# Seven quarter products in place of eight for the second matrix product of six batches, all batches unrolled

## The chip, the core and the metric

The kernel runs on one core of a Trainium2 chip. The metric is device time in microseconds (us), and lower is better. TensorE (PE) does the matrix products, VectorE (DVE) and ScalarE (ACT) the elementwise work, SyncE (SP) issues nearly all transfers, and GpSimd (POOL) prepares a few constants.

## The reference, cut to what matters

```
y    = x @ weight[adapter_ids]^T            # per batch: 256 x 1024 times 1024 x 1024
base = y @ W_up^T                           # 256 x 1024 times 1024 x 1024
top1 = argmax(y @ gate_w^T + expert_bias)   # one of 4 experts for each token
d    = (y @ lora_A^T, the 8 columns of top1) @ lora_B^T of top1
out  = x + base + d
```

There are 8 batches of 256 tokens and a hidden size of 1024. Everything is float32.

## The kernel before, in words

TensorE takes its operands as fp32r, a rounded form. To keep float32 accuracy each operand is split into hi (the rounded copy, made by ACT) and lo (the rest, made by DVE as raw minus hi), and a product is three: hi times hi, hi times lo, lo times hi. So each of the two large products of a batch costs three passes.

**First product.** For each of 8 blocks of 128 output features (`c`) it takes one 512 KB block of the batch's adapter weights from a ring of four raw blocks `w_raw` (split into `w_hi`, `w_lo`, rings of four too). For each of 8 slices `k` it issues a matmul of 512 columns (w_hi times x hi and x lo, L474) and one of 256 (w_lo times x hi, L476) into one of two PSUM banks. Then ACT copies one half of the bank out (`y_small`, L292), DVE adds the other (`y_full`, L408), ACT rounds it (`y_hi`, L296) and DVE takes the rest (`y_lo`, L413). Between these, ACT and DVE split the weights that come next (L271, L352) and, after the last block, the next batch's x (L257, L339). TensorE may go on with block `c` when `y_full` of block `c - 2` is done and the weights of `c` are split.

**Second product.** For each of two tiles of 128 tokens (`t`) three PSUM banks hold 366, 366 and 292 output columns; the third also holds 2 x 36 columns of lora_A and the gate (hi and lo), appended to `up_hi`. `bank_ab` (L485) feeds the first two with matmuls of 366 columns, `bank_c` (L494) the third with 364, 328 and 292. From the third bank DVE chooses the expert and builds `z_parts` (`choose`), TensorE transposes it (L502), ACT copies that back (`zT`, L313), and `add_lora` (L509) adds the LoRA term to each bank. DVE adds the banks to the rows of x (`finish`, L400) and SP stores them.

Batch 0 is written out, also splitting w_up once; batches 1 to 7 run in a loop. Every engine works its own list in order and waits on semaphores at fixed places; that order is written by hand. SP's list matters below: a load of a raw block waits until the block that it overwrites has been split by DVE, and everything behind it in SP's list waits too.

Of the kernel before, what the change touches and what calls it, by code (L numbers as in the profile page):

```python
# [8 lines left out]

# [1 line left out]

# [2 lines left out]

P = 128
F32 = mybir.dt.float32
F32R = mybir.dt.float32r  # L20
I32 = mybir.dt.int32
ALU = mybir.AluOpType
AX_X = mybir.AxisListType.X


def build(nc, xT, x, ids, w, w_up, gl, lora_b, bias, out):
    B, S, H = x.shape
    KC = H // P
# [7 lines left out]
    NW = H + 2 * GL  # L36
    RING = 4
    HALVES = 2
    HK = KC // HALVES
    XQ = 4  # L40
    XK = KC // XQ
    XD = 2
    QUARTERS = 4
    QK = KC // QUARTERS
    WARM = 18
    LAST = (2, 1, 0)

    UP_EARLY = OC // 2

    CUT = (NW // 3 + 1) // 2 * 2  # L50
    BANK_C = H - 2 * CUT
    STEPS = 8
    assert T == 2 and 4 * ER == P and BANK_C + 2 * GL <= 512 and B >= 3

    with ExitStack() as ctx:
# [19 lines left out]
        def sem(name):  # L75
            return ctx.enter_context(nc.semaphore(name))

        w_raw = sb("w_raw", [P, RING, KC * P])
        w_hi = sb("w_hi", [P, RING, KC * P], F32R)
        w_lo = sb("w_lo", [P, RING, KC * P], F32R)  # L80
        x_raw = sb("x_raw", [P, KC, S])
        x_hilo = sb("x_hilo", [P, KC, 2 * S], F32R)
        up_hi = sb("up_hi", [P, OC, NW], F32R)
        up_raw, up_lo = sb_over("up_raw", "up_lo", [P, OC, H])
        gl_raw = sb("gl_raw", [P, OC, GL])
        y_small = sb("y_small", [P, 2, S])
        y_full = sb("y_full", [P, 2, S])
        y_hi = sb("y_hi", [P, OC, S], F32R)
        y_lo = sb("y_lo", [P, OC, S], F32R)
        rows = sb("rows", [P, T, H])  # L90
        lb_raw = sb("lb_raw", [P, H])
        lb_parts = sb("lb_parts", [P, H], F32R)
        warm_f, warm = sb_over("warm_f", "warm", [P, 2 * S])
        bias_sb = sb("bias_sb", [P, E])
        rank = sb("rank", [P, E])
        eye_f = sb("eye_f", [P, P])
        eye = sb("eye", [P, P], F32R)
        zlo = sb("zlo", [P, T, GL])
        zg = sb("zg", [P, T, GL])
        lg = sb("lg", [P, T, E])  # L100
        lmax = sb("lmax", [P, T])
        score = sb("score", [P, T, E])
        smax = sb("smax", [P, T])
        zm = sb("zm", [P, T, ER])
        z_parts = sb("z_parts", [P, T, P], F32R)
        zT = sb("zT", [P, T, P], F32R)

        ps_y = [ctx.enter_context(nc.psum_tensor(f"ps_y{i}", [P, 512], F32)) for i in range(2)]
        ps_o = [ctx.enter_context(nc.psum_tensor(f"ps_o{t}", [P, 3, 512], F32)) for t in range(T)]

        x_raw_in = [sem(f"x_raw_in{d}") for d in range(XD)]
        w_raw_in = [sem(f"w_raw_in{s}") for s in range(RING)]
        up_raw_in = [sem(f"up_raw_in{c}") for c in range(OC)]
# [3 lines left out]
        bias_in = sem("bias_in")  # L117
        x_hi_ready = sem("x_hi_ready")
        x_ready = sem("x_ready")
        w_hi_ready = sem("w_hi_ready")  # L120
        w_ready = sem("w_ready")
        up_hi_ready = sem("up_hi_ready")
        up_ready = sem("up_ready")
        gl_hi_ready = sem("gl_hi_ready")
# [3 lines left out]
        warm_step = sem("warm_step")  # L128
        warm_ready = sem("warm_ready")
# [3 lines left out]
        y_done = sem("y_done")  # L133
        y_small_ready = sem("y_small_ready")
        y_full_ready = sem("y_full_ready")
        y_hi_ready = sem("y_hi_ready")
        y_ready = sem("y_ready")
        z_done = sem("z_done")
# [5 lines left out]
        out_ready = sem("out_ready")  # L144
# [3 lines left out]


        @block.sync  # L150
        def _(sp):
            def adapter(b):

                i = sp.value_load(ids[0:1, b:b + 1] if isinstance(b, int) else ids[0:1, bass.ds(b, 1)])  # L154
# [5 lines left out]
            def load_w(b, c, i):  # L160
                if not (isinstance(b, int) and b == 0 and c < RING):

                    sp.wait_ge(w_ready, (b * OC + c - RING + 1) * QUARTERS)
                sp.dma_start(w_raw[:, c % RING, :], w[bass.ds(i * OC + c, 1), :, :].rearrange("a p n -> (a p) n")  # L164
                             ).then_inc(w_raw_in[c % RING], 16)

            def load_x(b, d):
                sp.wait_ge(x_ready, (b - 1) * XQ + (d + 1) * (XQ // XD))
                ks = slice(d * (KC // XD), (d + 1) * (KC // XD))
                sp.dma_start(x_raw[:, ks, :], xT[b, :, ks, :]).then_inc(x_raw_in[d], 16)  # L170

            def load_up(c):
                sp.dma_start(up_raw[:, c, :], w_up[c, :, :]).then_inc(up_raw_in[c], 16)

            def load_rows(b, t):
                if not (isinstance(b, int) and b == 0):

                    sp.wait_ge(stored[t], b * 16 * (t + 1))
                sp.dma_start(rows[:, t, :], x[b, t * P:(t + 1) * P, :]).then_inc(rows_in[t], 16)

            def store_rows(b, t):
                toks = slice(t * P, (t + 1) * P)
                if t == 0:
                    sp.wait_ge(out_ready, b * 6 + 3)
                    sp.dma_start(out[b, toks, :], rows[:, t, :]).then_inc(stored[t], 16)
                else:
                    sp.wait_ge(out_ready, b * 6 + 5)
                    sp.dma_start(out[b, toks, CUT:], rows[:, t, CUT:]).then_inc(stored[t], 16)
                    sp.wait_ge(out_ready, b * 6 + 6)
                    sp.dma_start(out[b, toks, 0:CUT], rows[:, t, 0:CUT]).then_inc(stored[t], 16)  # L190

            i = adapter(0)
            for c in range(RING):
                load_w(0, c, i)
            for c in range(RING, OC):
                load_w(0, c, i)
                load_up(c - RING)
            sp.dma_start(gl_raw[:, :, :], gl[:, :, :]).then_inc(gl_in, 16)
            for c in range(RING, OC):
                load_up(c)  # L200
            for d in range(XD):
                load_x(1, d)
# [3 lines left out]
            i = adapter(1)  # L206
            for c in range(RING):
                load_w(1, c, i)
            for t in range(T):
                load_rows(0, t)  # L210
            with sp.Fori(0, B - 2) as b:
                i = adapter(b + 1)
                for c in range(RING, OC):
                    load_w(b + 1, c, i)
                for d in range(XD):
                    load_x(b + 2, d)
                for t in range(T):
                    store_rows(b, t)
                i = adapter(b + 2)
                for c in range(RING):  # L220
                    load_w(b + 2, c, i)
                for t in range(T):
                    load_rows(b + 1, t)
            i = adapter(B - 1)
            for c in range(RING, OC):
                load_w(B - 1, c, i)
            for t in range(T):
                store_rows(B - 2, t)
            for t in range(T):
                load_rows(B - 1, t)  # L230
            for t in range(T):
                store_rows(B - 1, t)
            for t in range(T):
                sp.wait_ge(stored[t], B * 16 * (t + 1))


        @block.gpsimd
        def _(pool):
# [3 lines left out]
                               base=0, pattern=[[-1, P]], channel_multiplier=1).then_inc(eye_step, 1)  # L242
            for e in range(E):
                pool.memset(rank[:, e:e + 1], float(E - e)).then_inc(rank_ready, 1)

            pool.wait_ge(gl_hi_ready, 1)
            pool.tensor_tensor(up_hi[:, :, H + GL:NW], gl_raw[:, :, :], up_hi[:, :, H:H + GL].bitcast(F32),
                               ALU.subtract).then_inc(gl_ready, 1)


        @block.scalar
        def _(act):
            def x_hi(b, q):
                if not (isinstance(b, int) and b == 0):
                    act.wait_ge(y_done, b * OC)
                act.wait_ge(x_raw_in[q * XD // XQ], (b + 1) * 16)
                act.copy(x_hilo[:, q * XK:(q + 1) * XK, 0:S], x_raw[:, q * XK:(q + 1) * XK, :]  # L257
                         ).then_inc(x_hi_ready, 1)
# [6 lines left out]
            def w_hi_part(b, c):  # L265
                if not (isinstance(b, int) and b == 0 and c < RING):
                    act.wait_ge(y_done, b * OC + c - RING + 1)
                act.wait_ge(w_raw_in[c % RING], (b * (OC // RING) + c // RING + 1) * 16)  # L268
                for h in range(HALVES):
                    part = slice(h * HK * P, (h + 1) * HK * P)  # L270
                    act.copy(w_hi[:, c % RING, part], w_raw[:, c % RING, part]  # L271
                             ).then_inc(w_hi_ready, QUARTERS // HALVES)

            def up_hi_part(c):
                act.wait_ge(up_raw_in[c], 16)
                act.copy(up_hi[:, c, 0:H], up_raw[:, c, :]).then_inc(up_hi_ready, 1)

            def gate_hi():
                act.wait_ge(gl_in, 16)
# [320 lines left out]
```

## Time and profile before

| | |
|---|---|
| median of 3 runs | 389.05 us (388.99 to 389.36) |
| the profiled execution | 389.27 us, its span 387.5 us |
| PE busy | 381.2 us of the span, 2258 matmuls |
| DVE busy | 212.2 us |
| ACT busy | 144.9 us |
| DMA | 63.7 MB, mean 164 GB/s |

The span runs from the first to the last instruction; 1.8 us of the profiled execution lie around it. Busy times of different engines overlap, so they don't add up.

### The profile page before, as it was taken

How to read it: one execution, taken by the hardware profiler on the slowest of the kernel's cores; microseconds unless marked ns; L12 is line 12 of the kernel's file. 1: busy time of each engine (PE TensorE's matmuls, PEld its weight loads, DVE VectorE, ACT ScalarE, POOL GpSimd, SP SyncE). 2: the span in 40 equal slices, each digit the busy share in tenths (PEclk: the TensorE clock that was granted, in tenths of full speed). 3: DMA queues.
4: the chain of work that ended last, by engine and by line, in shares of the span. 5: the costliest groups of instructions: out<-in, count | busy, mean ns of one | idle time of the engine just before them, and what ended most of it. 6: DMA issues, size and time to landing. Idle time of an engine off the chain costs nothing.

```text
span 387.5 us, 6808 instructions
## 1 busy us (share of the span) xinstructions
PE 381.2 (98%) x2258; PEld 356.3 (92%) x2258; DVE 212.2 (55%) x493; ACT 144.9 (37%) x318; POOL 1.7 (0%) x11
## 2 busy tenths in 40 slices
PE   7999999999999999999999999999999999999996
PEld 5789998899988999889998999989998899988996
DVE  4776976463564554735737347455365562664132
ACT  5666905370063701536025440345204461054000
POOL 0000000000000000000000000000000000000000
PEclk9999999999999999999999999999999999999999
DMA  7999459702775118643096332872338703540002
GB/s 244 355 415 292 175 208 297 255 7 102 188 251 210 67 41 246 236 167 108 31 277 201 140 108 75 260 247 68 108 123 262 250 15 108 184 141 0 0 0 110
DMA packets 18921, 63.70 MB, mean 164 GB/s; under 512 B 2272, under 2 KB 3424, under 8 KB 18912
## 3 DMA queue, kind: packets, MB, share of 16 engines
q1 hardware_dynamic: 18624, 62.55, 48.2%
q10 hardware_dynamic: 288, 1.05, 0.8%
q8 instruction: 3, 0.05, 0.1%
q14 instruction: 6, 0.05, 0.0%
HBM read 55.20 MB, written 8.39 MB: 164 GB/s over the span
## 4 chain that ended last, share of the span: by engine, by line
PE 95%; DMA 2%; SPq 1%; DVE 1%; issue 0%; ACT 0%; DVEq 0%; ACTq 0%
PE ps_o L485 34%; PE ps_y L474 30%; PE ps_o L494 15%; PE ps_y L476 15%; PE ps_o L509 2%; DMA w_raw<-w_dram 2%; SPq L154 1%; DVE w_lo L352 1%; SPq L164 0%; PE ps_y L502 0%; ACT w_hi L271 0%; DVE rows L400 0%; DVE y_full L408 0%; DVEq L350 0%; ACTq L268 0%
## 5 line engine op out<-in xcount | busy, mean ns | idle before, releaser
L474 PE MATMUL ps_y<-x_hilo,w_hi 128*128 128x512 f32 x512 | 178.8, 395 | 1.2 <-DVE y_full L408 0.6
L476 PE MATMUL ps_y<-x_hilo,w_lo 128*128 128x256 f32 x512 | 142.3, 278 | 0.0
L474 PEld LDWEIGHTS ps_y<-x_hilo,w_hi 128*128 128x128 f32 x512 | 96.0, 188 | 24.3 <-DVE w_lo L345 1.0
L476 PEld LDWEIGHTS ps_y<-x_hilo,w_lo 128*128 128x128 f32 x512 | 96.3, 188 | 0.0
L352 DVE TENSOR_TENSOR w_lo<-w_raw,w_hi 128x512 fp32r<-128x512 f32 x126 | 80.1, 687 | 7.6 <-ACT w_hi L271 7.2
L485 PE MATMUL ps_o<-up_hi,y_hi 128*128 128x366 f32 x256 | 75.0, 334 | 0.0
L485 PE MATMUL ps_o<-up_lo,y_hi 128*128 128x366 f32 x256 | 74.1, 330 | 0.0
L485 PE MATMUL ps_o<-up_hi,y_lo 128*128 128x366 f32 x256 | 74.0, 330 | 0.0
L271 ACT CAST w_hi<-w_raw 128x512 fp32r<-128x512 f32 x126 | 69.9, 620 | 4.8 <-DMA w_raw<-w_dram 4.7
L292 ACT COPY y_small<-ps_y 128x256 f32<-128x256 f32 x64 | 23.9, 373 | 114.4 <-PE ps_y L476 114.4
L408 DVE TENSOR_TENSOR y_full<-ps_y,y_small 128x256 f32<-128x256 f32 x64 | 27.1, 424 | 64.2 <-ACT y_small L292 64.2
L485 PEld LDWEIGHTS ps_o<-up_lo,y_hi 128*128 128x128 f32 x256 | 47.0, 189 | 0.0
L485 PEld LDWEIGHTS ps_o<-up_hi,y_lo 128*128 128x128 f32 x256 | 46.9, 188 | 0.0
L485 PEld LDWEIGHTS ps_o<-up_hi,y_hi 128*128 128x128 f32 x256 | 45.4, 188 | 0.4
L494 PE MATMUL ps_o<-up_hi,y_hi 128*128 128x364 f32 x128 | 40.9, 329 | 0.0
L494 PE MATMUL ps_o<-up_hi,y_lo 128*128 128x328 f32 x128 | 38.9, 312 | 0.0
L313 ACT CAST zT<-ps_y 128x128 fp32r<-128x128 f32 x16 | 4.3, 267 | 91.5 <-PE ps_y L502 91.5
L494 PE MATMUL ps_o<-up_lo,y_hi 128*128 128x292 f32 x128 | 37.9, 296 | 0.0
L413 DVE TENSOR_TENSOR y_lo<-y_full,y_hi 128x256 fp32r<-128x256 f32 x64 | 27.0, 422 | 15.1 <-ACT y_hi L296 15.1
L400 DVE TENSOR_TENSOR rows<-ps_o,rows 128x366 f32<-128x366 f32 (+1 forms) x48 | 21.5, 506 | 22.3 <-PE ps_o L509 22.3
L296 ACT CAST y_hi<-y_full 128x256 fp32r<-128x256 f32 x64 | 26.0, 406 | 18.8 <-DVE y_full L408 18.8
L377 DVE COPY zlo<-ps_o 128x36 f32<-128x36 f32 x16 | 3.1, 195 | 50.5 <-PE ps_o L494 50.5
(38 smaller groups left out, 198.6 us busy)
## 6 DMA issues: line engine op xcount, KB each, us to landing
w_raw<-w_dram SPq DMA_DIRECT2D x64, 512.0 KB, 4.2
rows<-x_dram SPq DMA_DIRECT2D x16, 512.0 KB, 5.2
x_raw<-xT_dram SPq DMA_DIRECT2D x14, 512.0 KB, 8.1
up_raw<-w_up_dram SPq DMA_DIRECT2D x8, 512.0 KB, 9.6
out_dram<-rows SPq DMA_DIRECT2D x8, 512.0 KB, 8.6
out_dram<-rows SPq DMA_DIRECT2D x8, 329.0 KB, 7.9
out_dram<-rows SPq DMA_DIRECT2D x8, 183.0 KB, 7.0
x_raw<-xT_dram ACTq DMA_DIRECT2D x2, 512.0 KB, 4.3
```

Source lines behind the costliest of these rows:

```text
L271: act.copy(w_hi[:, c % RING, part], w_raw[:, c % RING, part]).then_inc(w_hi_ready, QUARTERS // HALVES)
L292: act.copy(y_small[:, c % 2, :], ps_y[c % 2][:, S:2 * S]).then_inc(y_small_ready, 1)
L296: act.copy(y_hi[:, c, :], y_full[:, c % 2, :]).then_inc(y_hi_ready, 1)
L352: dve.tensor_tensor(w_lo[:, c % RING, part], w_raw[:, c % RING, part], w_hi[:, c % RING, part].bitcast(F32), ALU.subtract).then_inc(w_read ...
L400: dve.tensor_tensor(rows[:, t, part], ps_o[t][:, k, 0:part.stop - part.start], rows[:, t, part], ALU.add).then_inc(out_ready, 1)
L408: dve.tensor_tensor(y_full[:, c % 2, :], ps_y[c % 2][:, 0:S], y_small[:, c % 2, :], ALU.add).then_inc(y_full_ready, 1)
L413: dve.tensor_tensor(y_lo[:, c, :], y_full[:, c % 2, :], y_hi[:, c, :].bitcast(F32), ALU.subtract).then_inc(y_ready, 1)
L474: pe.matmul(ps_y[c % 2][:, :], w_hi[:, c % RING, cols], x_hilo[:, k, :], start=(k == 0), stop=False)
L476: last = pe.matmul(ps_y[c % 2][:, S:2 * S], w_lo[:, c % RING, cols], x_hilo[:, k, 0:S], start=False, stop=(k == KC - 1))
L485: pe.matmul(ps_o[t][:, k, 0:CUT], y[:, c, toks], up[:, c, k * CUT:(k + 1) * CUT], start=(c == 0 and n == 0), stop=False)
L494: last = pe.matmul(ps_o[t][:, 2, 0:end - 2 * CUT], y[:, c, toks], up[:, c, 2 * CUT:end], start=(c == 0 and end == NW), stop=(c == OC - 1 a ...
L509: pe.matmul(ps_o[t][:, k, 0:part.stop - part.start], zT[:, t, :], lb_parts[:, part], start=False, stop=True, skip_group_check=(k == 2)).th ...
```

## The change

w_up (transposed) is seen as four quarters of 512 x 512 (B11, B12, B21, B22), y as four quarters of 128 tokens x 512 features (A11, A12, A21, A22). Batches 0 and 1 (`b < PLAIN`) form the product from eight quarter products, batches 2 to 7 from seven, by Strassen's algorithm in the form with four sums on each side: S1 to S4 are sums of y's quarters, made anew in each batch by DVE, and T1 to T4 sums of w_up's, made once during batches 1 and 2 from quarters that SP loads a second time. Each quarter product is 4 slices of three matmuls, all of 512 columns (`quarter`). The seven share four PSUM banks: what several outputs have in common is accumulated in `ps_u`, which DVE adds to the rows at intermediate states. The small product with lora_A and the gate is one of its own: 16 matmuls of 256 columns with the 72 hi and lo columns as weights (`gates`), and 4 of 36 columns that fold and transpose it (`logits`).

The ring of raw weight blocks shrinks from four to three (`RAWS`), that of the split ones stays four (`RING`). x_raw shares memory with the lo half of `x_hilo`, so the next x is loaded only when the first product is over. All loops are unrolled. No loop is left on any engine.

The core of the diff, with some calls drawn together in one line and comments added on the right; the code that it replaces is printed above:

```
+    RAWS = 3
     RING = 4
+    def splits_at(b, c):
+        if b == 0:
+            return (c + RAWS,) if c + RAWS < OC else ()
+        n = b * OC + c + RING
+        if c < OC - RING or (b == 1 and c < 6) or (b > PLAIN and c < OC - 1):
+            return (n,) if n < BLOCKS else ()
+        return ()
+    def splits_after(b):
+        done = [n for c in range(OC) for n in splits_at(b, c)]
+        first = done[-1] + 1
+        return range(first, min((b + 1) * OC + RING, BLOCKS))
...
SyncE
+            def load_w(n, i):
+                if n >= RAWS:
+                    sp.wait_ge(w_ready, (n - RAWS + 1) * QUARTERS)
+                sp.dma_start(w_raw[:, n % RAWS, :], ...
...
ScalarE
+            def first_product(b):
+                for c in range(OC):
+                    y_small(b, c)
+                    for n in splits_at(b, c):
+                        w_hi_part(n)
+                    if c == 4:
+                        act.wait_ge(y_full_ready, b * OC + Q)
+                        y_hi_part(A11)
+                        if b < PLAIN:
+                            y_hi_part(A21)
...
+            def plain(b):
...
+                g_parts(b)
+                for q in range(XQ):
+                    x_hi(b + 1, q)
+                for n in splits_after(b):
+                    w_hi_part(n)
+                z_back(b)
+            def strassen(b):
...
+                if b > PLAIN:
+                    for n in splits_after(b):
+                        w_hi_part(n)
+                x_hi(b + 1, 0); x_hi(b + 1, 1)
+                g_parts(b)
+                x_hi(b + 1, 2); x_hi(b + 1, 3)
+                if b == PLAIN:
+                    for n in splits_after(b):
+                        w_hi_part(n)
+                z_back(b)
...
VectorE
+            def plain(b):
...
+                g_full(b)
+                g_lo_part(b)
+                for q in range(XQ):
+                    x_lo(b + 1, q)
+                choose(b)
+                for n in splits_after(b):
+                    w_lo_part(n)
+                for i, (t, j) in enumerate(((0, 0), (0, 1), (1, 0), (1, 1))):
+                    add_row(b, t, j, ps_plain[t, j])
+            def strassen(b):
+                y_add(S2, A22, S3, ALU.subtract, slice(Q - 1, Q))
+                y_lo_part(b, 2, S3)
+                y_add(S4, A12, S2, ALU.subtract)
+                y_add(S1, A21, A22, ALU.add)
+                y_lo_part(b, 3, S2)
+                add_row(b, 0, 0, ps_u)                    # product 1 done
+                y_lo_part of A12, S1, A22, S4
+                add_row(b, 1, 1, ps_v)                    # product 2 done
+                if b == PLAIN:
+                    t_lo(T4, 1)
+                else:
+                    for n in splits_after(b):
+                        w_lo_part(n)
+                add_row(b, 1, 0, ps_u)                    # product 3 done
+                x_lo(b + 1, 0); x_lo(b + 1, 1)
+                g_full(b)
+                g_lo_part(b)
+                x_lo(b + 1, 2); x_lo(b + 1, 3)
+                choose(b)
+                add_row(b, 1, 1, ps_u, after=2)           # product 5 done
+                if b == PLAIN:
+                    for n in splits_after(b):
+                        w_lo_part(n)
+                add_row of ps_l, ps_p, ps_v, and at last ps_u
...
TensorE
+            def quarter(ps, p, q, k, start, stop):        # hi*hi, hi*lo, lo*hi, 512 columns each
...
+            def plain(b):
+                for c in range(OC):
+                    term(0, 0, c)
+                    term(0, 1, c)
+                    term(1, 0, c)
+                    if c == Q:
+                        gates(b)
+                    if c == Q + 1:
+                        logits(b)
+                for c in range(Q):
+                    term(1, 1, c)
+                transpose_z(b)
+                for c in range(Q, OC):
+                    term(1, 1, c)
+                    if c == Q + 1:
+                        add_lora(b, 0, 0, ...), (b, 0, 1, ...), (b, 1, 0, ...)
+                add_lora(b, 1, 1, ps_plain[1, 1])
+            def strassen(b):
+                product(b, 1, ps_u, A11, B11, True)
+                product(b, 2, ps_v, S3, T3, True)
+                product(b, 3, ps_u, S2, T2, False)
+                gates(b)
+                product(b, 4, ps_p, A12, B21, True)
+                logits(b)
+                product(b, 5, ps_u, S1, T1, False)
+                product(b, 6, ps_v, A22, T4, False)       # transpose_z after its slice 1
+                add_lora(b, 1, 1, ps_l, True)             # waits for z_back's second copy
+                add_lora(b, 0, 0, ps_p)
+                add_lora(b, 1, 0, ps_v)
+                add_lora(b, 0, 1, ps_u)
+                product(b, 7, ps_u, S4, B22, False, True)
```

Blocks of adapter weights are numbered through, `n = 8 b + c`. `w_hi_part(n)` needs block `n` landed; `w_lo_part(n)` needs that; `load_w(n + 3)` needs `w_lo_part(n)`. By `splits_after`, batches 0 and 2 split four blocks during the second product (8 to 11, and 24 to 27), batch 1 two (18, 19), batches 3 to 6 one each, batch 7 none.

## Rows read from the trace of the kernel before

**Rows 1.** The page's part 1: busy time, share of the span, count.
```profile
PE 381.2 (98%) x2258; PEld 356.3 (92%) x2258; DVE 212.2 (55%) x493; ACT 144.9 (37%) x318; POOL 1.7 (0%) x11
```

**Rows 2.** The page's part 4: who stands on the chain that ended last.
```profile
PE 95%; DMA 2%; SPq 1%; DVE 1%; issue 0%; ACT 0%; DVEq 0%; ACTq 0%
```

**Rows 3.** Windows: first and second product of batches 0, 1, 2 (one missing).
```profile
8.68:32.22 23.54, 22.88 (x129) 19.64 (x129) 17.53 (x33) 15.02 (x33) 0.81 (x1) 1.00 1.01 372
32.22:57.20 24.98, 24.98 (x157) 24.89 (x156) 20.96 (x42) 14.71 (x25) 0.00 (x0) 1.00 0.63 209
57.20:79.59 22.39, 22.39 (x129) 19.44 (x128) 12.49 (x27) 9.21 (x22) 0.00 (x0) 1.00 0.76 251
79.59:103.95 24.36, 24.36 (x153) 24.36 (x152) 13.83 (x37) 7.57 (x16) 0.00 (x0) 1.00 0.31 90
103.95:126.31 22.36, 22.36 (x130) 19.58 (x130) 11.31 (x23) 9.22 (x22) 0.00 (x0) 1.00 0.66 231
```

**Rows 4.** Chain that ended last, second product of batch 1: start, us, what.
```profile
90.82 4.05 PE ps_o L494 x27
...
99.92 4.03 PE ps_o L485 x24
```

**Rows 5.** Timeline of PE: first product of batch 2, pairs 2 and 32.
```profile
104.31 0.40 PE L474 MATMUL ps_y<-x_hilo,w_hi 128*128 128x512 f32 x1
...
114.70 0.40 PE L474 MATMUL ps_y<-x_hilo,w_hi 128*128 128x512 f32 x1
```

**Rows 6.** Timeline of PE, warm-up matmuls: the first ten; the tenth to the seventeenth.
```profile
1.95 4.29 PE L460 MATMUL ps_y<-warm 128*128 128x512 f32 x10 [1.95 <-DVE warm L439]
...
5.84 2.02 PE L460 MATMUL ps_y<-warm 128*128 128x512 f32 x8
```

**Rows 7.** Timeline of PE, second product of batch 1: a transpose and what follows.
```profile
98.35 0.22 PE L502 MATMUL ps_y<-eye,z_parts 128*128 128x128 f32 x1
98.41 0.38 PE L485 MATMUL ps_o<-up_hi,y_hi 128*128 128x366 f32 x1
98.63 0.33 PE L485 MATMUL ps_o<-up_lo,y_hi 128*128 128x366 f32 x1
```

**Rows 8.** Groups of DVE by form: count, busy us, mean ns.
```profile
L408 DVE TENSOR_TENSOR y_full<-ps_y,y_small 128x256 f32<-128x256 f32 x64 | 27.1, 424 | 64.2 <-ACT y_small L292 64.2
L400 DVE TENSOR_TENSOR rows<-ps_o,rows 128x366 f32<-128x366 f32 x32 | 16.3, 533 | 22.3 <-PE ps_o L509 22.3
```

**Rows 9.** Timelines of DVE and ACT in batch 1: splits back to back.
```profile
83.86 2.49 DVE L352 TENSOR_TENSOR w_lo<-w_raw,w_hi 128x512 fp32r<-128x512 f32 x4
...
82.88 4.27 ACT L271 CAST w_hi<-w_raw 128x512 fp32r<-128x512 f32 x8
```

**Rows 10.** Timeline of DVE: first and last of the nine steps of choose.
```profile
94.92 0.20 DVE L377 COPY zlo<-ps_o 128x36 f32<-128x36 f32 x1 [1.56 <-PE ps_o L494]
...
96.73 0.22 DVE L392 TENSOR_TENSOR z_parts<-zm,z_parts 128x64 fp32r<-128x64 f32 x1
```

**Rows 11.** View of w_raw: from issue to landing.
```profile
DMA to landing us min/median/max: 3.1/4.2/13.4
```

**Rows 12.** Timeline of ACT, batch 0: waits for blocks 5, 6 and 7.
```profile
18.12 1.14 ACT L271 CAST w_hi<-w_raw 128x512 fp32r<-128x512 f32 x2 [1.99 <-DMA w_raw<-w_dram]
...
20.66 1.14 ACT L271 CAST w_hi<-w_raw 128x512 fp32r<-128x512 f32 x2 [0.82 <-DMA w_raw<-w_dram]
...
23.22 1.14 ACT L271 CAST w_hi<-w_raw 128x512 fp32r<-128x512 f32 x2 [0.84 <-DMA w_raw<-w_dram]
```

**Rows 13.** Timeline of all engines at the end of the span.
```profile
384.06 0.33 PE L509 MATMUL ps_o<-lb_parts,zT 128*128 128x366 f32 x1
384.43 0.54 DVE L400 TENSOR_TENSOR rows<-ps_o,rows 128x366 f32<-128x366 f32 x1 [2.58 <-PE ps_o L509]
```

More of the change, by code:

```diff
@@ L84, in build @@
[L84 to L89, printed above, removed]
+        x_at = place([P, 2, KC, S])
+        x_raw = nc.alloc_sbuf_tensor_at("x_raw", [P, 2, KC, S], F32, offset=x_at)
+        x_hilo = nc.alloc_sbuf_tensor_at("x_hilo", [P, 2, KC, S], F32R, offset=x_at)
+        up_stage, up_hi = sb_over("up_stage", "up_hi", [P, PARTS, Q, HALF])
@@ L172, in load_up @@
[L172 to L185, printed above, removed]
-                else:
[L187 to L190, printed above, removed]
+            def load_w(n, i):
+                if n >= RAWS:
+                    sp.wait_ge(w_ready, (n - RAWS + 1) * QUARTERS)
+                sp.dma_start(w_raw[:, n % RAWS, :], w[bass.ds(i * OC + n % OC, 1), :, :].rearrange("a p n -> (a p) n")
+                             ).then_inc(w_raw_in[n % RAWS], 16)
@@ L311, in batch, with z_back @@
+            def z_back(b):
                 for t in range(T):
@@ L323, in _ @@
             x_hi(0, XQ - 1)
-            for q in range(XQ // 2, QUARTERS):
+            for q in range(QUARTERS // 2, QUARTERS):
                 first_w_hi(q)
-            for c in range(1, RING):
-                w_hi_part(0, c)
-            batch(0, first=True)
-            with act.Fori(1, B - 1) as b:
-                batch(b)
-            batch(B - 1, last=True)
+            for n in range(1, RAWS):
+                w_hi_part(n)
+            for b in range(B):
+                first_product(b)
+                if b < PLAIN:
+                    plain(b)
+                else:
+                    strassen(b)
@@ L488, in bank_c @@
-            def bank_c(t, c):
-                toks = slice(t * P, (t + 1) * P)
-                terms = [(y_hi, up_hi, NW), (y_hi, up_lo, H), (y_lo, up_hi, H + GL)]
-                for y, up, end in terms if c < OC - 1 else terms[::-1]:
-                    last = pe.matmul(ps_o[t][:, 2, 0:end - 2 * CUT], y[:, c, toks], up[:, c, 2 * CUT:end],
-                                     start=(c == 0 and end == NW), stop=(c == OC - 1 and end == NW))
-                if c == OC - 1:
-                    last.then_inc(z_done, 1)
@@ new lines, in logits, with transpose_z @@
+            def logits(b):
+                if b == 0:
+                    pe.wait_ge(eye_ready, 2)
+                pe.wait_ge(g_ready, b + 1)
+                for t in range(T):
+                    for part in (g_hi, g_lo):
+                        last = pe.matmul(ps_z[:, t * GL:(t + 1) * GL], part[0:2 * GL, t, :], fold[0:2 * GL, :],
+                                         start=(t == 0 and part is g_hi), stop=False, skip_group_check=True)
+                last.then_inc(z_done, 1)
+            def transpose_z(b):
+                for t in range(T):
+                    pe.wait_ge(z_parts_ready, b * T + t + 1)
+                    pe.matmul(ps_y[t][:, 0:P], z_parts[:, t, :], eye[:, :], start=True, stop=True
+                              ).then_inc(zt_done, 1)
@@ L566 @@
+            warm_up()
+            for b in range(B):
+                first_product(b)
+                if b < PLAIN:
+                    plain(b)
+                else:
+                    strassen(b)
 def kernel(x, itok_B_3_7, L0_cond_weight, L0_ffn_W_up, L0_ffn_gate_w, L0_ffn_expert_bias, L0_ffn_lora_A,
```

760 lines of the change are left out of this document (488 added, 272 removed).

## The prediction

> **What bounds the kernel now.** The page's busy times come first: PE is busy for 98% of the span, DVE for 55% [rows 1]. Since matmuls overlap in the records, a busy PE proves nothing yet; the chain that ended last does, with 95% on PE and 2% on DMA [rows 2]. So time changes by what TensorE has to stream and by what makes it wait. The windows give the price of a stage: after batch 0 a first product takes 22.36 to 22.39 us, a second one 24.36, without idle time [rows 3].
>
> What sets PE's pace is the number of columns. 27 matmuls of `bank_c` (mean 328 columns) take 4.05 us, 150 ns each, 24 of 366 columns 4.03 us, 168 ns each [rows 4]. Thirty pairs of 512 + 256 columns take 114.70 - 104.31 = 10.39 us, 346 ns a pair [rows 5]. All lie at 0.45 to 0.46 ns a column. The only matmuls of 512 columns in a row are the last warm-up ones: from 5.84 on, eight take 2.02 us; less the last one's 0.39, seven starts lie 233 ns apart [rows 6]. Two thirds of a pair is 231. I take 232 ns for 512 columns and 116 for 256. A transpose takes 60 ns and makes the next matmul 50 ns longer [rows 7].
>
> **What the seven products are worth.** A Strassen batch issues 7 x 4 x 3 = 84 matmuls of 512 columns (19.49 us), 16 of `gates` (1.86), 4 of `logits` (0.24, at the price of a transpose, since no row shows 36 columns; at 116 ns it would be 0.2 more), 2 transposes with what follows (0.22) and 4 of LoRA (0.93): 22.74 us in place of 24.36. That is 1.62 less, in six batches 9.7 us. The saving is so small because the gate columns rode in `bank_c` for half of that price.
>
> A plain batch has 96 of 512 (22.27) and the same rest (3.25): 25.52 us. Batch 1 gains 1.16 us of work over its 24.36, batch 0 0.54 over its 24.98 [rows 3].
>
> The page "TensorE: Matmul & The Clock Gate" of the Trainium skill (section "Wait — 56ns, not 53.3ns?") puts a matmul at its columns over 2.4 GHz plus 2.5 ns, some 216 ns for 512. The rows show 232, and the measurement decides. By the page's price the two sides would shrink together, to an estimated 20.9 and 22.5 us, and the gain of a batch would be 1.6 again.
>
> **First products.** The matmuls are the same ones and the split ring is as deep. In batch 0 PE lost 0.66 us of 23.54 [rows 3]. There the smaller raw ring moves loads: a w_up block now goes ahead of block 3. Blocks 5, 6 and 7 came 2.5 us apart with a w_up block between them, 1.3 us for 512 KB [rows 12]; two more such blocks ahead of block 7 make it land some 2.6 us later, near 25.7, still before PE wants it at 28.5. But ACT waits for it ahead of `y_small` of block 5, which makes `y_full` late for PE by 0.7 us, about what the shorter list before the first block gives back. I take 0 for batch 0's first product, between -0.7 and +1.5.
>
> **Where PE will wait.** Batches 0 and 2 split four blocks during the second product, but there are three raw buffers. The fourth block can be loaded only when the first of the four is split by DVE, and both engines stand behind it: ACT does `w_hi` of the fourth before `z_back`, whose copies PE needs for `add_lora`. Durations: DVE splits 512 columns in 0.69 us, 0.60 in a row, ACT in 0.62 and 0.52 [rows 9]; a load takes at least 3.1 us [rows 11]; `choose` 2.03 us for one tile [rows 10], I take 2.5 for two in one chain, with more steps.
>
> *Batch 0*, from the end of `gates`: g's four steps 0.16 + 4 x 0.4 + gaps = 1.9 us; the four `x_lo` end at 4.3 (behind ACT's four `x_hi`, begun at 1.4); `choose` 6.8; `w_lo(8)` 8.1; block 11 lands 11.25; `w_hi(11)` 12.4; first zT 12.7. PE in that time has 9 + 18 + 12 + 6 = 45 matmuls of 512 columns (10.4), logits and transposes (0.5): it arrives at 10.9 and waits 1.8 us.
>
> *Batch 2*, from the start of product 1: PE does products 1 to 3 (8.35), gates (10.2), product 4 (13.0), logits, product 5 (16.1). DVE waits for that, adds a row (16.3 to 17.0, by 533 ns for 366 columns [rows 8], 0.69 for 512), and only then does `w_lo(24)` (18.2). Block 27 lands at 21.4, `w_hi(27)` ends at 22.5, the second zT at 23.0. PE has finished product 6 and the transposes at 19.0 and waits 4.0 us. Behind its wait stand the four LoRA matmuls and product 7, and behind them the whole next batch; nothing covers it. If the load took the median 4.2 us [rows 11] both waits would be 1.1 us longer; if PE's other waits are longer they shrink.
>
> Batch 1 has no such trap: blocks 18 and 19 are there before ACT reaches them. Its first product shares the DMA queues with 3 MB of w_up quarters and 1 MB of stores, but at 1.3 us for 512 KB the blocks still arrive within the ring's slack. DVE's `y_full(5)` in batch 1 comes within 0.3 us of need behind two y_lo and a `t_raw`; I count 0.
>
> **Strassen batches 3 to 7.** DVE feeds PE here step by step, so I followed each wait from the start of product 1. `y_full(7)` ends at 1.0 (ACT's and DVE's 0.4 each after the last matmul, [rows 8]), S2's last slice 1.35, `y_lo` of S3 2.0; product 2 wants it at 2.8. S4, S1 and `y_lo` of S2 end at 3.9, `add_row` at 4.5; product 3 wants both at 5.6. Four `y_lo` end at 7.0; gates want them at 8.35. Then rows, one split block, another row: 9.6; x_lo 10.8; g_full to g_lo 12.1; logits want it at 13.0. Two x_lo and `choose` end at 15.9; the transposes want it at 17.5. ACT's zT come at 18.1, LoRA wants them at 19.0. Each wait ends 0.8 to 1.5 us early, so nothing is added. DVE has some 34 us of work in 45, and each first product needs a block every 2.8 us with three buffers, against 3.1 to 4.2 us for a load: a block has 8.4 us.
>
> **The tail.** The last row is 512 columns in place of 366, 0.69 us against 0.54 [rows 13], and its store is 256 KB, not 183: +0.3 us. Unrolling is worth nothing: at the loop's turn PE had no idle time [rows 3].
>
> **The sum:** -9.7 + 1.2 + 0.5 + 0 + 1.8 + 4.0 + 0.3 = -1.9 us. The profiled execution (389.27, 0.2 above the median) would be 387.4, and the median 389.05 - 1.9 = 387.1 us, which I predict.
>
> **Rivals.**
>
> 1. *The waits don't come* (DVE or SP is earlier than I reckon, or block 11 and 27 land in time). For it: loads of 3.1 us exist, and only 4 us separate the case from mine. Against it: DVE's list puts `w_lo(24)` behind product 5 whatever the load takes. 387.1 - 5.8 = 381.3 us; half of it, 384.
>
> 2. *The array slows down after the long wait.* The rows show that it can run at half pace: the first ten warm-up matmuls start (5.84 - 1.95) / 9 = 432 ns apart, the next 233, so 3.9 us of work passed at half pace after idleness, a loss of 1.9 us [rows 6]. No wait in this trace is longer than 0.7 us once work has begun, so no row tells whether 4.0 us are enough. With it: 387.1 + 1.9 = 389.0 us, no change; with both waits followed by it, 390.9. The page "TensorE: Matmul & The Clock Gate" (section "HAM oscillation — how this bites in real kernels") says that a long enough wait between bursts of matmuls puts the array back to its lower clock, and that the work after it then runs at half rate. By that rule this rival comes true; the trace agrees only in that the start is at half pace.
>
> 3. *DVE falls behind in every Strassen batch*, at the place with least slack: `y_lo` of S3 before product 2, or `g_lo` before logits. It decides from 0.45 us a batch on (2.7 us over six). That needs DVE 1.3 us later than reckoned, for instance if its strided sums or the reads of PSUM cost half as much again. At 1 us a batch 387.1 + 6 = 393 us. Against it: fp32 elementwise work has one price per column in all rows [rows 8, 9].
>
> 4. *The change does not stream less*: if 512 columns cost more than 232 ns by the time that y's quarters are the weights. Each ns is 84 x 6 + 192 = 0.7 us; the two rows that bound it lie 2 ns apart, so +-1.5 us.
>
> **How the numbers follow.** A measurement of this kernel can tell about 0.2% (0.8 us) from no change. My forecast, with waits between 4 and 8 us: 0.46. Rival 1: 0.19. Rival 2: 0.18. Rival 3 and other lateness: 0.14. Rival 4 beyond its bound: 0.03. Faster by over 0.2% (below 388.3): 0.40 of the forecast, all of rival 1, 0.05 of rival 2, 0.02 of the rest, 0.66. Within 0.2%: 0.04 + 0.10 + 0.02 = 0.16. Slower: 0.02 + 0.03 + 0.13 = 0.18. The range takes in rivals 1 and 2, 380.8 to 390.2, and leaves out some 0.18; the likeliest case alone spans 385.5 to 388.5.
>
> **What would show it.** In the profile after: L-rows of the three `quarter` matmuls with starts 232 ns apart; a second product of 22.7 us in batches 3 to 7 with PE idle below 0.3 us; in batch 2 one idle stretch of PE of about 4 us ahead of an `add_lora` matmul, released by ACT's zT copy, and in ACT a wait of some 5 us for DMA `w_raw`; one of about 2 us in batch 0. Whether PE's matmuls after those waits stand 232 or 430 ns apart decides rival 2. Idle time of PE in each of batches 3 to 7, released by DVE, would be rival 3. The prediction is wrong if both waits are missing, or if a wait that I passed as early enough is not.

## The result: 1.5% slower, and the profile after

| | before | after |
|---|---|---|
| median | 389.16 us (4 runs) | 394.92 us (4 runs, 394.15 to 395.66) |
| ratio | | 1.0148, 95% interval 1.013 to 1.0167 |
| profiled execution | 389.27 us, span 387.5 | 394.15 us, span 392.2 |

The forecast was 387.1 us and faster. The measured time lies 7.8 us above it, outside the range of 380.8 to 390.2. Page of the kernel after, parts 1 and 4 (compare [rows 1, 2]):

```profile
PE 379.0 (97%) x1946; PEld 320.9 (82%) x1946; DVE 263.4 (67%) x501; ACT 163.0 (42%) x329; POOL 4.0 (1%) x15
...
PE 83%; DMA 8%; ACT 3%; DVE 3%; issue 1%; SPq 1%; ACTq 0%; DVEq 0%
```

PE still looks full, but on the chain its share fell from 95% to 83%, and DMA has 8% where it had 2%. So 12% of the span, some 47 us, has moved from PE to transfers, ACT and DVE on the chain, though PE is busy for most of that time too. The windows show what it costs: first and second product of batches 0 to 3, each from its first matmul. Columns are the stretch, its length, the busy time (with the number of instructions) of PE, weight loads, DVE, ACT and POOL, then granted clock, DMA share, GB/s.

```profile
8.87:31.81 22.94, 22.84 (x130) 19.60 (x128) 16.14 (x28) 13.46 (x28) 0.00 (x0) 1.00 0.98 384
31.81:59.16 27.35, 25.72 (x125) 21.09 (x123) 22.89 (x39) 16.29 (x29) 2.65 (x2) 1.00 0.55 166
59.16:85.76 26.60, 24.36 (x129) 20.82 (x128) 15.27 (x26) 9.88 (x21) 0.00 (x0) 0.94 0.87 322
85.76:111.20 25.44, 25.44 (x125) 21.20 (x123) 19.45 (x36) 10.80 (x19) 0.00 (x0) 1.00 0.28 92
111.20:133.81 22.61, 22.61 (x130) 19.60 (x129) 15.69 (x25) 11.51 (x21) 0.00 (x0) 1.00 0.64 233
133.81:162.47 28.66, 24.53 (x112) 20.10 (x111) 21.90 (x46) 10.63 (x22) 0.00 (x0) 0.94 0.38 127
162.47:185.07 22.60, 22.60 (x129) 19.61 (x128) 14.35 (x25) 11.12 (x23) 0.00 (x0) 1.00 0.58 211
185.07:207.74 22.67, 22.67 (x112) 19.04 (x111) 16.66 (x38) 7.52 (x16) 0.00 (x0) 1.00 0.31 103
```

Batches 4 to 7 repeat the last two rows. The same cut for batch 2 of the kernel before. In [rows 3] I had set the end of its first product 0.16 us too late, inside the second product:

```profile
103.95:126.15 22.20, 22.20 (x129) 19.42 (x129) 11.31 (x23) 9.22 (x22) 0.00 (x0) 1.00 0.67 232
126.15:150.66 24.51, 24.51 (x154) 24.51 (x153) 13.83 (x37) 7.57 (x16) 0.00 (x0) 1.00 0.28 88
```

The seven products do save: 24.51 - 22.67 = 1.84 us a batch. Three things eat it. PE waits for 1.6, 2.2 and 4.1 us (who PE waited for, in total, times, longest):

```profile
PE ps_l L806 <- ACT zT L388: 4.1, 1, 4.1
PE ps_y L762 <- DVE y_raw L546: 2.2, 1, 2.2
...
PE ps_u L806 <- ACT zT L388: 1.6, 1, 1.6
```

Behind the two longer waits the granted clock is 0.50, that is 1.2 GHz in place of 2.4. These are the windows of the two dips:

```profile
79.47:82.88 3.41, 3.41 (x12) 2.84 (x12) 3.41 (x7) 1.53 (x4) 0.00 (x0) 0.50 0.87 263
158.00:161.40 3.40, 3.40 (x10) 2.63 (x9) 1.53 (x3) 0.00 (x0) 0.00 (x0) 0.50 0.84 301
```

PE's timeline at the second: after the wait the first matmuls start 0.33, 0.24 and 0.23 us apart, later 0.43, and after the dip 0.24 again. So PE ran for 0.9 us at full clock after the wait before the clock fell, and each dip costs half of its 3.4 us, 1.7.

```profile
152.59 0.40 PE L773 MATMUL ps_v<-up_hi,y_parts 128*128 128x512 f32 x1
157.11 0.50 PE L806 MATMUL ps_l<-lb_parts,zT 128*128 128x512 f32 x1 [4.13 <-ACT zT L388]
157.44 0.40 PE L806 MATMUL ps_p<-lb_parts,zT 128*128 128x512 f32 x1
157.68 0.39 PE L806 MATMUL ps_v<-lb_parts,zT 128*128 128x512 f32 x1
...
158.69 0.63 PE L771 MATMUL ps_u<-up_lo,y_parts 128*128 128x512 f32 x1
159.12 0.63 PE L773 MATMUL ps_u<-up_hi,y_parts 128*128 128x512 f32 x1
```

ACT's timeline gives the cause of both waits. In each, ACT stands 5 to 6 us for a raw block (15 and 27, counted through), and what PE needs comes after it in ACT's list (`y_small` of the batch's block 4 at 77.14; zT at 156.63):

```profile
76.10 1.14 ACT L356 CAST w_hi<-w_raw 128x512 fp32r<-128x512 f32 x2 [5.07 <-DMA w_raw<-w_dram]
77.14 0.36 ACT L371 COPY small<-ps_y 128x256 f32<-128x256 f32 x1
...
155.59 1.14 ACT L356 CAST w_hi<-w_raw 128x512 fp32r<-128x512 f32 x2 [6.03 <-DMA w_raw<-w_dram]
156.63 0.43 ACT L388 CAST zT<-ps_y 128x128 fp32r<-128x128 f32 x2
```

The third thing is small and everywhere: a first product of batches 2 to 7 takes 22.60 us where it took 22.20 before.

**Where the 4.7 us of span come from** (after minus before, each from its first matmul; the stages of before not shown above are 23.54 and 24.60 in batch 0, 22.60 and 24.53 in batch 1, 24.51 for the second and 22.20 for the first product in all later ones): batch 0 -0.6 and +2.75; batch 1 +4.0 and +0.9; batch 2 +0.4 and +4.15; batches 3 to 7 5 x (+0.4 - 1.84) = -7.2; start and end +0.3. Sum 4.7.

### The profile page after: what moved, and what is told of

It reads as the page before. It is cut to its first block, busy times and chain, and to the rows that moved or that the text cites. A ratio compares the mean times of both kernels' runs of the same rounds, so it can differ in the third digit from the quotient of the medians.

```text
span 392.2 us, 5419 instructions
## 1 busy us (share of the span) xinstructions
PE 379.0 (97%) x1946; PEld 320.9 (82%) x1946; DVE 263.4 (67%) x501; ACT 163.0 (42%) x329; POOL 4.0 (1%) x15
## 4 chain that ended last, share of the span: by engine, by line
PE 83%; DMA 8%; ACT 3%; DVE 3%; issue 1%; SPq 1%; ACTq 0%; DVEq 0%
PE ps_y L762 25%; PE ps_y L764 13%; DMA w_raw<-w_dram 8%; PE ps_u L769 7%; PE ps_u L771 6%; PE ps_u L773 6%; PE ps_g L782 4%; PE ps_v L769 3%; PE ps_v L773 3%; PE ps_v L771 3%; PE ps_p L769 2%; PE ps_p L771 2%; PE ps_p L773 2%; ACT w_hi L356 2%; DVE w_lo L501 2%
## 5 line engine op out<-in xcount | busy, mean ns | idle before, releaser
L371 ACT COPY small<-ps_y 128x256 f32<-128x256 f32 x64 | 23.8, 372 | 115.4 <-PE ps_y L764 115.3
L546 DVE TENSOR_TENSOR y_raw<-ps_y,small 128x256 f32<-128x256 f32 x64 | 27.1, 423 | 53.0 <-ACT small L371 52.9
L769 PE MATMUL ps_u<-up_hi,y_parts 128*128 128x512 f32 x112 | 45.2, 404 | 0.0
L771 PE MATMUL ps_u<-up_lo,y_parts 128*128 128x512 f32 x112 | 44.3, 396 | 0.0
L773 PE MATMUL ps_u<-up_hi,y_parts 128*128 128x512 f32 x112 | 44.2, 394 | 0.0
L557 DVE TENSOR_TENSOR y_parts<-y_raw,y_parts 128x512 fp32r<-128x512 f32 x50 | 32.8, 691 | 1.5 <-ACT y_parts L374 0.9
L374 ACT CAST y_parts<-y_raw 128x512 fp32r<-128x512 f32 x50 | 28.9, 620 | 9.6 <-DVE y_raw L552 9.6
L773 PEld LDWEIGHTS ps_u<-up_hi,y_parts 128*128 128x128 f32 x112 | 21.4, 191 | 4.8
L769 PE MATMUL ps_v<-up_hi,y_parts 128*128 128x512 f32 x64 | 25.3, 395 | 0.0
L773 PE MATMUL ps_v<-up_hi,y_parts 128*128 128x512 f32 x64 | 25.1, 392 | 0.0
L769 PEld LDWEIGHTS ps_u<-up_hi,y_parts 128*128 128x128 f32 x112 | 21.4, 191 | 4.4
L771 PE MATMUL ps_v<-up_lo,y_parts 128*128 128x512 f32 x64 | 24.9, 389 | 0.0
L771 PEld LDWEIGHTS ps_u<-up_lo,y_parts 128*128 128x128 f32 x112 | 21.5, 192 | 3.9
```

The source lines that it names most:

```text
L371: act.copy(small[:, c % 2, :], ps_y[c % 2][:, S:2 * S]).then_inc(y_small_ready, 1)
L374: act.copy(y_parts[:, p, :, 0, :], y_raw[:, p, :, 1, :]).then_inc(y_hi_ready, 1)
L546: dve.tensor_tensor(y_raw[:, p:p + 2, c % Q, 1, :], ps_y[c % 2][:, 0:S].rearrange("p (t n) -> p t n", t=T), small[:, c % 2, :].rearrange(" ...
L557: dve.tensor_tensor(y_parts[:, p, :, 1, :], y_raw[:, p, :, 1, :], y_parts[:, p, :, 0, :].bitcast(F32), ALU.subtract).then_inc(y_ready, 1)
L769: pe.matmul(ps[:, :], y_parts[:, p, k, 0, :], up_hi[:, q, k, :], start=start, stop=False, skip_group_check=True)
L771: pe.matmul(ps[:, :], y_parts[:, p, k, 0, :], up_lo[:, q, k, :], start=False, stop=False, skip_group_check=True)
```

## The experiments

My theory after the result: two orders (z_back behind the fourth split; 3 MB of w_up quarters ahead of block 15) and the dips that they set off explain batches 0 to 2. The slower first products had no explanation at first. Ratios are to the kernel before in the same comparison. In the edits `-` and `+` are against the changed kernel, or where said against the kernel before.

**1. z_back before the fourth split**, in `plain` of ScalarE, and the same in `strassen` for batch 2:

```
-                for n in splits_after(b):
+                for n in splits_after(b)[:3]:
                     w_hi_part(n)
                 z_back(b)
+                for n in splits_after(b)[3:]:
+                    w_hi_part(n)
```

> ACT copies zT back (z_back) before it takes up the fourth of the four blocks that batches 0 and 2 split in their second product; nothing else changes. Theory (the changed kernel loses 1.9 us in batch 0 and 4.3 us in batch 2 because z_back stands behind a block whose load begins only after the first of the four is split, and the clock dip right behind the second wait costs another 1.7 us): both waits of PE ahead of add_lora vanish, no granted clock below 1 between 150 and 165 us, second product of batch 2 is 22.7 us and of batch 0 25.4 us, 392.2 - 7.9 = 384.3 us of span, some 387 us. Rival (z_back is late for another reason, for instance the transposes or choose): the waits stay within 0.5 us of 1.9 and 4.3 and the time within 1 us of 394.9. Rival 2 (the dip comes from the free course of the chip, not from the wait): the waits vanish, a dip stays, some 389 us.

388.56 us, ratio 0.9977 (0.9956 to 0.9997); 387 was expected. Both waits are gone and the second product of batch 2 runs through at full clock:

```profile
134.10:156.81 22.71, 22.71 (x112) 19.05 (x111) 18.94 (x42) 10.53 (x22) 0.00 (x0) 1.00 0.28 88
```

So the rivals of this run fall. The missing part is in batch 1: PE comes to it earlier and now waits 3.4 us there in place of 2.2, with the dip behind it. The transfers, not PE, set the time in that stretch: block 15 lands at 76.4 us of the span here and at 76.0 in the changed kernel, though PE began the batch 0.8 us earlier. The ten executions are not alike: two have a mean granted clock of 1.000, so no dip, and took 387.7 and 387.8 us, the others 0.991 to 0.996.

**2. T2's quarters after blocks 15 and 16**, in SyncE:

```
-            load_stage(T2, 0, 0)
...
                 for n in early[:2]:
                     load_w(n, i)
+                if b == 1:
+                    load_stage(T2, 0, 0)
                 load_rows(b)
```

> SP issues one of the three pairs of w_up quarters (T2's, 1 MB) after adapter blocks 15 and 16 and not before them. Theory (in batch 1 block 15 lands 11.4 us after its issue because 3 MB of quarters and 1 MB of stores stand ahead of it; PE then waits 2.2 us at block 6 and runs at half clock for 3.4 us, 1.7 us lost): block 15 lands some 2.6 us earlier, PE waits under 0.3 us there, no dip near 80 us, first product of batch 1 22.6 us in place of 26.6, time 394.9 - 4.0 = 391 us. Rival (the block is late because of the transfers' own slowness or of stores, or DVE's t_raw is what makes PE wait): the wait stays over 1.5 us and the time within 1 us of 394.9.

391.66 us, ratio 1.0068 (1.0047 to 1.0088). The dip in batch 1 is gone, the wait is 0.6 us there (1.2 us over three waits in all), and the gain is 3.3 us of the 4 expected. Block 15 landed 7.8 us after its issue in place of 11.4. ACT still stood 1.5 us for it and 1.0 us for block 16:

```profile
72.99 1.14 ACT L357 CAST w_hi<-w_raw 128x512 fp32r<-128x512 f32 x2 [1.49 <-DMA w_raw<-w_dram]
...
75.39 1.14 ACT L357 CAST w_hi<-w_raw 128x512 fp32r<-128x512 f32 x2 [0.99 <-DMA w_raw<-w_dram]
```

The wait that is left hangs on block 16. Between the two issues SP reads the next batch's adapter number, for 3.2 us on the chain, and then the chain (start, us, what) has the load of block 16:

```profile
69.50 5.80 DMA w_raw<-w_dram
```

Behind block 16 DVE's list has two `y_lo` and the 1.2 us sum for T3 (`t_raw`) before the `y_full` that PE wants, the place that the prediction had put within 0.3 us of need.

**3. The wait of batch 2 filled**, in TensorE, ahead of the LoRA matmuls:

```
+                if first:
+                    for _ in range(36):
+                        pe.matmul(ps_z[:, 256:512], eye[:, :], lb_parts[:, 0:256], start=True, stop=True)
                 add_lora(b, 1, 1, ps_l, True)
```

> 36 extra matmuls of 256 columns (identity times part of lora_B, into an unused half of the ps_z bank; their result is read by nobody) fill the wait of PE in batch 2, between product 6 and the LoRA matmuls. They take 36 x 0.117 = 4.2 us, as long as the wait. Theory (the wait of 4.1 us is what makes the chip grant half the clock for the next 3.4 us): no dip in batch 2, add_lora starts at the same place, time lower by 1.7 us, 393.2. Rival (the clock falls for another reason): the dip stays, time 394.9 or up to 1 us more. The wait itself is not removed in either case.

391.64 us, ratio 1.0060 (1.0042 to 1.0078), with no dip in the profiled execution. The second product of batch 2, and 3.5 us of it around the LoRA matmuls and behind them, where the changed kernel has its second dip:

```profile
132.52:159.75 27.23, 27.20 (x149) 23.35 (x148) 21.90 (x46) 10.64 (x22) 0.00 (x0) 1.00 0.36 118
...
155.90:159.40 3.50, 3.47 (x16) 2.85 (x16) 2.44 (x4) 0.01 (x1) 0.00 (x0) 1.00 0.72 256
```

The batch's second product is 1.4 us shorter though PE still can't go on with useful work. So the idle time is what lets the clock fall. The gain is 3.3 us and not 1.7 because batch 1 had no dip in this run either: its longest wait was 1.5 us there. The edit touches nothing before batch 2, so that half of the gain is not its doing; block 15 landed 9.1 us after its issue in this execution, with the same order of transfers that gave 11.4 and, in experiment 1, 12.5.

**4. Layout of x in the kernel before**, against it:

```
-        x_hilo = sb("x_hilo", [P, KC, 2 * S], F32R)
+        x_hilo = sb("x_hilo", [P, 2, KC, S], F32R)
```

> The kernel before with one edit: x_hilo is laid out with the hi half of all slices first and the lo half 8 KB behind, as in the changed kernel, in place of hi and lo side by side; the matmul of 512 columns then reads two runs of 256. Theory (this layout is why a first product takes 22.60 us after the change and 22.20 before, with the same matmuls): first products of 22.6 us, second ones unchanged, 389.1 + 8 x 0.4 = 392.3 us. Rival (unrolled code, the smaller raw ring or other addresses slow the first product): first products stay at 22.2 us, time within 0.5 us of 389.1.

389.35 us, ratio 0.9992 (0.9983 to 1.0002), and the first product of batch 2 is unchanged:

```profile
104.03:126.24 22.21, 22.21 (x129) 19.41 (x129) 11.31 (x23) 9.21 (x22) 0.00 (x0) 1.00 0.72 233
```

My theory of the layout falls. (All accesses to x_hilo were changed to match.)

**5. TensorE's loop written out in the kernel before**, against it (one test in `first_product` now also asks for `b == 0`, which the numbers from 1 on need):

```
-            with nc.Fori(1, B, engines=(mybir.EngineType.PE,), hint_back_edge=True) as b:
+            for b in range(1, B):
                 batch(b)
```

> The kernel before with TensorE's loop over batches 1 to 7 written out; the other engines keep their loops, and the matmuls and waits are the same. In the kernel before, pairs of 512 + 256 columns start 349, 350, 361 ns after each other in the loop's first pass (first product 22.60 us) and 343, 350 in the later ones (22.20); in the changed kernel all batches have the slower pattern. Theory (TensorE's instructions stream more slowly when they are run for the first time, so written-out code costs 6 ns a pair, 0.4 us a batch): the six first products of batches 2 to 7 take 22.60 us, time 389.4 + 2.4 = 391.8 us. Rival (the pattern comes from where the tiles lie or from the other engines): they stay at 22.20, time within 0.5 us of 389.4.

389.61 us, ratio 1.0007 (0.9996 to 1.0018). The first products stay at 22.21 us:

```profile
103.97:126.18 22.21, 22.21 (x130) 19.41 (x129) 11.31 (x23) 9.21 (x22) 0.00 (x0) 1.00 0.67 232
```

The theory of first-run code falls too, and with it any cost of the unrolling of PE.

**6. The w_up quarters before blocks 11 to 14**, in SyncE:

```
+            load_stage(T3, 0, 1)
+            load_stage(T2, 0, 0)
+            load_stage(T1, 1, 1)
             for n in range(OC + RAWS, OC + RAWS + RING):
                 load_w(n, i)
-            load_stage(T3, 0, 1)
-            load_stage(T2, 0, 0)
-            load_stage(T1, 1, 1)
```

> The changed kernel, with the three pairs of w_up quarters (3 MB) issued before adapter blocks 11 to 14 and not after them, so that they land while SP and the DMA queues would else wait for the split of block 8. Theory (PE's 2.2 us wait in batch 1, and the dip behind it, come from block 15 standing behind these 3 MB): block 15 lands within 5 us of its issue, no wait of PE over 0.2 us in batch 1's first product, no dip there, 394.9 - 4.0 = 390.9 us. Rival (stores and rows, or DVE's sums, hold PE up): over 1 us of wait stays, over 393 us.

390.92 us, ratio 1.0043 (1.0028 to 1.0058), as expected. Block 15 landed 3.3 us after its issue, and the first product of batch 1 takes 22.61 us without a wait. The profiled execution shows more: in batch 2 the same wait of 4.0 us was followed by a dip twice as long, and batch 3's first product, which begins 0.6 us after it ends, took 22.19 us, the only one of the batches 1 to 7 at the faster pace. The window of that dip:

```profile
152.16:158.98 6.82, 5.99 (x14) 4.73 (x15) 3.18 (x5) 0.78 (x3) 0.00 (x0) 0.50 0.75 267
```

The mean granted clock over the span tells how common this is: 0.996 fits one dip of 3.4 us, 0.991 two of them or one of 6.8. Four of the eight executions have 0.990 or 0.991, four 0.996.

**7. The edits of experiments 1 and 6 together.**

> Both repairs together: z_back ahead of the fourth split in batches 0 and 2, and the w_up quarters before blocks 11 to 14. Theory: no wait of PE over 0.3 us after block 0 and no dip; span 392.2 - 7.9 - 4.0 = 380.3 us, time some 382.5 us, which is clearly below the 389.4 of the kernel before. Rival (the waits only move to a later place, so the seven products are worth less than 1.4 us a batch): 385 us or more.

382.76 us, ratio 0.9833 (0.9812 to 0.9854), 382.5 expected. After block 0 PE waits 0.2 us in all, and there is no dip. This is the change as it was meant: 1.7% faster than before. All four executions have a granted clock of 0.999 or 1.000.

**8. Both repairs, TensorE loops over batches 3 to 7** (the counts and places in the ring that it uses are written in terms of `b` and `c` for that):

```
+            with nc.Fori(PLAIN + 1, B, engines=(mybir.EngineType.PE,), hint_back_edge=True) as b:
+                first_product(b)
+                strassen(b)
```

> The two repairs, and TensorE alone takes batches 3 to 7 in a loop; the other engines stay written out. Theory (first-run code is slower): the first products of batches 4 to 7 take 22.20 us in place of 22.60, the second ones stay at 22.67 or fall by up to 0.3, time 1.6 to 2.8 us below the kernel with the two repairs alone. Rival (the layout and not the code sets the pattern): same time as that kernel within 0.3 us.

383.21 us, ratio 0.9847 (0.9828 to 0.9865): no gain, first products at 22.60 us in all passes. That settles it for TensorE's code.

**9 to 11. A different entry into the first product.** The one fast batch of experiment 6 led to a new theory: the pace depends on how the first product is entered. PE's timeline in the changed kernel (batch 3) has pairs that start 0.35, 0.36, 0.35 us apart:

```profile
165.99 0.40 PE L762 MATMUL ps_y<-x_hilo,w_hi 128*128 128x512 f32 x1
...
166.34 0.40 PE L762 MATMUL ps_y<-x_hilo,w_hi 128*128 128x512 f32 x1
...
166.70 0.40 PE L762 MATMUL ps_y<-x_hilo,w_hi 128*128 128x512 f32 x1
...
167.05 0.40 PE L762 MATMUL ps_y<-x_hilo,w_hi 128*128 128x512 f32 x1
```

The edit to the kernel of experiment 7 (N is 128 or 366) and, with 512 columns after each batch of the loop, to the kernel before:

```
                 product(b, 7, ps_u, S4, B22, False, True)
+                pe.matmul(ps_y[0][:, 0:N], eye[:, :], lb_parts[:, 0:N], start=True, stop=True)
```

> The kernel with both repairs, and at the end of each batch from 2 on one extra matmul of 128 columns (its result is read by nobody) between product 7 and the next first product. Theory (the 349, 350, 361 ns pattern of the pairs is no matter of code or layout but of how weight loads and matmuls fall into step when a first product begins; in the run with the early w_up quarters alone batch 3 had the faster pattern right after a dip): a different entry puts at least some of the first products of batches 3 to 7 into the faster pattern, 22.2 us in place of 22.6; with all five, 2.0 - 0.3 = 1.7 us below the kernel with both repairs. Rival (something that lasts, such as the addresses of the tiles, sets the pattern): all stay at 22.60, time 0.3 us above it.

381.60 us, ratio 0.9800 (0.9779 to 0.9820). That is 1.2 us less than in experiment 7, which was measured in another comparison; the two intervals overlap, so the windows and not the times show the gain. The first products of batches 3 to 7 take 22.25 us, the second ones 0.06 more:

```profile
151.38:173.63 22.25, 22.25 (x131) 19.48 (x129) 16.39 (x29) 11.16 (x24) 0.00 (x0) 1.00 0.76 270
173.63:196.36 22.73, 22.73 (x114) 19.09 (x112) 17.21 (x39) 7.62 (x16) 0.00 (x0) 1.00 0.37 123
```

> As the run with 128 columns, but the extra matmul has 366, as the last one of a batch in the kernel before. Same theory: if the columns of the last matmul decide, this one has the faster pattern (22.2 us); cost of the extra matmuls 6 x 0.17 = 1.0 us. Rival: 22.60 everywhere.

384.27 us, ratio 0.9880 (0.9848 to 0.9911). With 366 columns the first products stay at 22.61 us. So the number of columns of the last matmul alone does not decide the pace; the kernel before enters with 366 as well and is fast.

> The kernel before, with one extra matmul of 512 columns (read by nobody) after each batch of the loop, so that a first product is entered as in the changed kernel. Theory of entry: first products of batches 2 to 7 change from 22.20 to 22.60 us, time 389.3 + 7 x 0.23 + 6 x 0.4 = 393.3 us. Rival (lasting cause): they stay at 22.20 and the time is 390.9 us.

394.46 us, ratio 1.0151 (1.0111 to 1.0191); 393.3 was expected and 390.9 by the rival. The profiled execution took 394.21 us with a span of 391.5, which is 4.0 above the span before, as expected; the other 2.7 us lie around it (1.8 before), and why is open. The kernel before, with nothing changed but one matmul ahead of each first product from batch 2 on, has the slower pace in all six:

```profile
104.38:126.99 22.61, 22.61 (x129) 19.62 (x128) 11.29 (x23) 9.21 (x22) 0.00 (x0) 1.00 0.65 227
126.99:151.75 24.76, 24.76 (x155) 24.72 (x154) 13.87 (x38) 7.57 (x16) 0.00 (x0) 1.00 0.29 94
```

Both directions are shown: one matmul ahead of the stream can bring the faster pace or the slower one. What falls into step is not known from these runs, nor is what decides it.

## Why the prediction was wrong, point by point

**What bounds the kernel**: right. Columns set the pace.

**The seven products**: right in kind. A Strassen batch's second product measured 22.67 us for my 22.74. Inside it the 84 matmuls start 227 ns apart, not 232; `logits` cost some 0.2 us more than I took. The saving came out as 1.84 us and not 1.62, but 0.15 of that is my late cut in [rows 3], which took time from the second product before (24.36 for 24.51) and gave it to the first. A plain batch measured 25.44 for 25.52. Rival 4 is out.

**Waits behind the fourth split**: right. Forecast 1.8 and 4.0 us, measured 1.6 and 4.1 (4.3 counted between matmul starts), removed by experiment 1 with that one order.

**Batch 1, the step that failed**: "Its first product shares the DMA queues with 3 MB of w_up quarters and 1 MB of stores, but at 1.3 us for 512 KB the blocks still arrive within the ring's slack." Block 15 landed 11.4 us after its issue (chain of the kernel after):

```profile
64.65 11.35 DMA w_raw<-w_dram
```

The price per load was not what failed. In that stretch the queues were full, at nearly the rate of batch 0 (384 GB/s there):

```profile
64.65:76.00 11.35, 11.35 (x66) 9.80 (x64) 3.86 (x7) 3.20 (x7) 0.00 (x0) 1.00 0.98 382
```

They moved 4.34 MB in the 11.35 us, 1.4 us for each 512 KB. What I had not counted is how many transfers stand before the block, and what the ring can bear. At the issue of block 15 four of the six pieces of the quarters and both stores were still to land (a fifth piece landed 0.05 us later); with the block that makes seven, 9.1 us by my price of 1.3, and parts of block 16 and of the rows, issued later, moved in the same time. PE wanted to go on at 76.27 and did so at 78.50, 2.5 us after the landing, because ACT stood for the block with `y_small` behind it. So the load had 9.1 us at most: by my own price there was no slack, and I had written "within the ring's slack" without a number for it. PE lost 2.2 us. Experiment 2 moved a third of the quarters and left 0.6 us (its theory allowed 0.3), experiment 6 moved them all and left nothing, as its theory said.

**The clock, the second step**: rival 2 came true behind the wait of 4.1 us, at 1.7 us (I had 1.9), and once more behind the 2.2 us of batch 1 that I had not forecast; behind the 1.6 us of batch 0 it did not. I gave it 0.18 because no row of before had a long wait. The page "TensorE: Matmul & The Clock Gate" of the Trainium skill (section "HAM oscillation — how this bites in real kernels") warned of it: after a long enough wait the next burst of matmuls runs at half rate. Experiment 3 agrees: with the idle time filled there is no dip. In the profiled executions, waits of 1.7 us and less (after the warm-up) had none behind them, waits of 2.2, 3.4 and 4.0 to 4.1 us had one each time.

**First products, the third**: "The matmuls are the same ones and the split ring is as deep" priced them as unchanged. They took 0.4 us more in batches 2 to 7, by the way that they are entered (experiments 9 and 11). In batch 1 the kernel before had 22.60 as well, which the windows of before would have shown: [rows 3] has 22.39 there because my cuts were late, by 0.38 us at its start and 0.17 at its end, so that it looked like the 22.36 of batch 2.

**Rivals 1 and 3** did not come. DVE was in time at every place of batches 3 to 7.

The misses add up, in the profiled execution with its forecast of 387.4: batch 1 4.1 (wait and dip), batch 2 2.2 (1.7 for the dip, 0.3 for the wait, 0.2 for the first product), batches 3 to 7 0.9, a start that came 0.2 later, less 0.6 for batch 0. That is 6.8, and the execution took 394.15. The 0.6 is luck: batch 0's first product took 22.94 us here, but 23.2 to 24.1 in the other profiled executions with the new order, on both sides of the 23.54 that I had taken.

## What to carry to other kernels

Where a ring of buffers is shallower than the work that is queued behind it, look in each engine's list for what stands behind the block that can't be there yet; a single move of a short copy was worth 1.6%. Issue bulk loads into the stretch where the queues are idle, not into the one that follows, and count the transfers that stand before a block against the time that it has. When a change adds an idle stretch to TensorE, put the clock's fall into the sum (1.7 us for each wait of 2.2 to 4.1 us here, and some 3 us for the one of experiment 6) and not among the small risks.

## What was not expected of the hardware

A stream of alternating 512- and 256-column matmuls has at least two stable paces on the same data and addresses, 346.9 and 353.3 ns a pair (22.20 and 22.61 us for 64). What precedes the stream picks one, and without a wait of PE it lasted for all 64 pairs. One 60 ns matmul bought 0.36 us a batch, and one of 512 columns in the kernel before cost 0.41 us a batch beyond its own time. The clock's fall does not keep to the wait: in the changed kernel it came 0.9 us after PE had resumed, in experiment 6 0.8 us before (PE busy for 5.99 of the dip's 6.82 us), and that dip lasted twice as long as the others.
